# The last tile stored in two halves by two queues, and the tile before it finished earlier

## Chip, core and metric

One NeuronCore of a Trainium2 chip runs the whole program. The metric is device time in microseconds of one execution, as the median of several runs. Engines named below: TensorE (matrix products), VectorE, ScalarE, GpSimd, and SyncE (SP), which here only starts DMAs. Each engine works through its own queue of instructions in order; they meet at semaphores, which one engine or DMA counts up and another waits for.

## What is computed

```python
w = weights[conditions]                        # (128, 32, 32), picked from 200
h = einsum('bct,bcd->bdt', x, w)               # x: (128, 32, 256), float32
u = square(relu(einsum('bsh,hi->bsi', h, up_w)))        # 256 -> 1024
shared = einsum('bsi,ih->bsh', u, down_w)               # 1024 -> 256
scale = top_k(einsum('bsh,he->bse', h, gate_w), 2).sum()
y = shared + einsum('bsh,hd->bsd', h, expert_weight) * scale
mu, var = mean(y), mean(square(y - mu))                 # over the 256
out = x + (y - mu) * rsqrt(var + 1e-5) * gamma + beta
```

The 128 x 32 rows of x are 4096 tokens of 256 numbers.

## The kernel before, in words

The 4096 tokens are 32 groups of 128 rows (`GROUPS`); four of them make a block (`TILES`, `BLOCKS` = 8). A group is also called tile n, n = 4 * block + t, with n from 0 to 31. TensorE runs blocks in a pipeline: while block j is projected up (`up`, L385), block j-1 is projected down (`down`, L406). There is a last pass, j = `BLOCKS`, with `down` alone: it does two halves for each of the tiles 28 to 31, after the late half of tile 27. Products are made in float32 out of a rounded part and a rest, which is why each operand has a `_hi` and a `_lo`.

What follows a `down` on the other engines, for each tile:

- VectorE, `total` (L571): waits for the matmuls (`down_done`), adds the two halves of the result and the expert part (L581, L584), and takes statistics with L587. For the very last tile everything is already summed in PSUM, so `total` is only the statistics, straight from `down_ps` (L576).
- VectorE, `moments` (L589): aggregates the statistics (L597) and centres and scales by gamma (L603), into `y[t % 2]`.
- GpSimd, `inverse_std` (L689): waits for L597 and raises the variance to the power -0.5 (L692), into `rstd[t % 2]`.
- VectorE, `finish` (L606): waits for L603 and L692 and makes the result with L614, into `result[:, j % 2, t, :]`, and counts `result_done` up.
- SP stores the result. Blocks 0 to 6 go out as a whole, 512 KB (`store`, L277). Block 7 goes out tile by tile, 128 KB each: L290 waits for `result_done` to reach n + 1, L291 starts the DMA. The order is fixed, tile 28, 29, 30, 31.

VectorE's order is written by hand in the loop at L646 to L668. For blocks 0 to 6, `finish` of a tile follows its own `moments`. For block 7 it is one tile behind: `moments` of tile t is followed by `finish` of t - 1, so VectorE doesn't stand and wait for GpSimd. The last `finish` (tile 31) is behind the loop, L669. Just ahead of it stands, at L666, `finish` of tile 30, after the statistics and the centring of tile 31.

ScalarE's part ends with `scale_moe` of the last tile (L533). At the end SP waits until all stores have landed (L292, L293; `result_moved`, one semaphore each for even and odd blocks), and the block is closed: every engine counts up a semaphore, and all leave together (L46).

Of the kernel before, what the change touches and what calls it, by code (L numbers as in the profile page):

```python
# [5 lines left out]
P = 128  # L6
# [29 lines left out]
def adaln_ffn(nc, x, cond, cond_w, gate_w, up_w, down_w, expert_w, gamma, beta, out):  # L36
# [9 lines left out]
    with ctx:  # L46
# [71 lines left out]
        wd_second_landed = [sem("wd_second_landed_sp"), sem("wd_second_landed_pool")]  # L118
        wd_landed = {j: sem(f"wd_landed_block{j}") for j in range(2, BLOCKS)}
        result_moved = [sem("result_moved_even"), sem("result_moved_odd")]  # L120


        warm_ready, consts_ready = map(sem, ("warm_ready", "consts_ready"))
# [108 lines left out]
        @block.sync  # L232
        def _(sp):
            def load_down(load):
                n = CH // DOWN_LOADS
                part = slice(n * load, n * (load + 1))
                sp.dma_start(down_raw[:, part, :], down_rows[:, part, :]).then_inc(down_landed[load], 16)

            cond_flat = cond.rearrange("(o b) -> o b", o=1)
            sp.dma_start(cond_row[:, 0:TILES * Q], cond_flat[:, 0:TILES * Q]).then_inc(cond_first_landed, 16)  # L240
            sp.dma_start(cond_row[:, TILES * Q:ROWS_B], cond_flat[:, TILES * Q:ROWS_B]).then_inc(cond_later_landed, 16)
            sp.wait_ge(cond_first_landed, 16)
            values = conditions(mybir.EngineType.SP, range(0, HALF_BLOCK))
            sp.wait_ge(wd_zeroed[0], 1)
            for b in BY_SP:
                sp.dma_start(square_of(b), weights_of(values[b])).then_inc(wd_first_landed[b // Q], 16)
            values = conditions(mybir.EngineType.SP, range(HALF_BLOCK, 2 * HALF_BLOCK))
            for b in BY_SP_LATER:
                sp.dma_start(square_of(b), weights_of(values[b])).then_inc(wd_later_landed[0], 16)
            load_up(sp, 2)  # L250
            sp.dma_start(eg_raw[:, :, 0:T], expert_w.rearrange("(k p) h -> p k h", p=P)).then_inc(eg_landed, 16)
            sp.dma_start(eg_raw[:, :, T:EG], gate_w.rearrange("(k p) e -> p k e", p=P)).then_inc(eg_landed, 16)
            sp.dma_start(x_sb[:, groups(1), :], x_rows[:, groups(1), :]).then_inc(x_landed[1], 16)
            sp.wait_ge(cond_later_landed, 16)
            second = range(TILES * Q, TILES * Q + HALF_BLOCK)
            values = conditions(mybir.EngineType.SP, second)
            sp.wait_ge(wd_zeroed[1], 1)
            for b, value in values.items():
                sp.dma_start(square_of(b), weights_of(value)).then_inc(wd_second_landed[0], 16)
            load_down(0)  # L260
            load_down(1)
            sp.dma_start(beta_b[:, :], beta.rearrange("(o t) -> o t", o=1).to_broadcast([P, T])) \
                .then_inc(ln_landed, 16)
            sp.dma_start(gamma_b[:, :], gamma.rearrange("(o t) -> o t", o=1).to_broadcast([P, T])) \
                .then_inc(ln_landed, 16)

            def fetch(j):
                if TILES * (j + 1) > GROUPS - CH:

                    sp.wait_ge(down_lo_ready, DOWN_PARTS)  # L270
                sp.dma_start(x_sb[:, groups(j), :], x_rows[:, groups(j), :]).then_inc(x_landed[j], 16)
                batches = range(TILES * Q * j, TILES * Q * (j + 1))
                values = conditions(mybir.EngineType.SP, batches)
                for b, value in values.items():
                    sp.dma_start(square_of(b), weights_of(value)).then_inc(wd_landed[j], 16)

            def store(j):  # L277
                sp.wait_ge(result_done, TILES * j + TILES)
                sp.dma_start(out_rows[:, groups(j), :], result[:, j % 2, :, :]).then_inc(result_moved[j % 2], 16)

            for j in range(2, BLOCKS - 2):
                fetch(j)
            store(0)
            for j in range(BLOCKS - 2, BLOCKS):
                fetch(j)
            for j in range(1, BLOCKS - 1):
                store(j)
            for t in range(TILES):
                n = TILES * (BLOCKS - 1) + t
                sp.wait_ge(result_done, n + 1)  # L290
                sp.dma_start(out_rows[:, n:n + 1, :], result[:, 1, t:t + 1, :]).then_inc(result_moved[1], 16)  # L291
            sp.wait_ge(result_moved[0], 16 * (BLOCKS // 2))  # L292
            sp.wait_ge(result_moved[1], 16 * (BLOCKS // 2 - 1 + TILES))  # L293

# [173 lines left out]
        @block.scalar  # L468
        def _(act):
            def hidden(j, k):  # L470
                act.wait_ge(hid_done, rounds(j, k))
                act.activation(hid_hi[:, j % 2, k, :], round_bank(j, k)[:, :], ACT.Copy).then_inc(hid_hi_done, 1)

            def hidden_first(half, k):
                act.wait_ge(hid_done, K * half + k + 1)
                act.activation(hid_hi[:, 0, k, half_tok(half)], first_bank(half, k)[:, 0:HALF_TOK], ACT.Copy) \  # L476
                    .then_inc(hid_hi_done, 1)

            def scale_moe(j, t):
                n = TILES * j + t  # L480
                act.wait_ge(scale_done, n + 1)
                to = moe_hl[:, 0, :] if last_tile(j, t) else moe[:, j % 2, t, :]
                act.activation(to, moe_ps[:, 0:T], ACT.Copy, scale=scale[:, t % 2:t % 2 + 1]) \  # L483
                    .then_inc(moe_scaled, 1)

            def rectify(j, c):
                n = CH * j + c
                act.wait_ge(up_done, n + 1)

                wait(act, square_done, n - 1)  # L490
                act.activation(relu[:, c % 2, :], up_ps[c % UPB][:, :], ACT.Relu).then_inc(relu_done, 1)  # L491
                act.wait_ge(relu_done, n + 1)
                act.activation(sq_hi[:, j % 2, c, :], relu[:, c % 2, :], ACT.Square).then_inc(sq_hi_done, 1)  # L493

            def split_up(part):
                act.wait_ge(up_landed[part], 16)
                act.activation(up_hi[:, :, split_cols(part)], up_raw[:, :, split_cols(part)], ACT.Copy) \
                    .then_inc(up_hi_ready, 1)

            def split_down(part):  # L500
                act.wait_ge(down_landed[part * DOWN_LOADS // DOWN_PARTS], 16)
                act.activation(down_hl[:, down_chunks(part), 0, :], down_raw[:, down_chunks(part), :], ACT.Copy) \
                    .then_inc(down_hi_ready, 1)


            act.activation(table_loaded[:, :], nc.const_aps.tensor(0.0, [P, 1], f32), ACT.Copy)
            load_x_first(act, 0)
            load_up(act, 0)
            act.wait_ge(cond_first_landed, 16)
            values = conditions(mybir.EngineType.Activation, range(0, HALF_BLOCK))  # L510
            act.wait_ge(wd_zeroed[0], 1)
            for b in BY_ACT:
                act.dma_start(square_of(b), weights_of(values[b])).then_inc(wd_first_landed[b // Q], 16)  # L513
            split_up(0)
            load_up(act, 1)
            load_x_first(act, 1)
            hidden_first(0, 0)
            hidden_first(0, 1)
            split_up(1)
            hidden_first(1, 0)  # L520
            hidden_first(1, 1)
            act.wait_ge(eg_landed, 32)
            act.activation(eg_hi[:, :, :], eg_raw[:, :, :], ACT.Copy).then_inc(eg_hi_ready, 1)
            for j in range(BLOCKS):
                for c in range(CH):
                    for moe_block, t in scaled_at(j, c):
                        scale_moe(moe_block, t)
                    for k in rounds_at(j, c - 1):
                        hidden(j + 1, k)
                    rectify(j, c)  # L530
                    for part in SPLIT_DOWN_AT.get(c, ()) if j == 0 else ():
                        split_down(part)
            scale_moe(BLOCKS - 1, TILES - 1)  # L533

        @block.vector
        def _(dve):
# [109 lines left out]
            for j in range(BLOCKS + 1):  # L646
                for c in range(CH):
# [12 lines left out]
                    for block, t in tiles_at(j, c):  # L660
                        moments(block, t)

                        if block < BLOCKS - 1:
                            finish(block, t)
                        elif t > 0:
                            finish(block, t - 1)  # L666
                    for part in SPLIT_DOWN_AT.get(c, ()) if j == 0 else ():
                        split_down(part)  # L668
            finish(BLOCKS - 1, TILES - 1)  # L669
# [77 lines left out]
```

## Time and profile before

| | us |
|---|---|
| median of 3 runs | 230.31 (230.11 to 230.64) |
| the profiled execution, its own time | 230.09 |
| its span, first to last instruction | 228.5 |

| engine | busy us | share of the span |
|---|---|---|
| TensorE, matmul | 221.8 | 97% |
| TensorE, weight load | 191.9 | 84% |
| VectorE | 162.2 | 71% |
| GpSimd | 130.5 | 57% |
| ScalarE | 105.7 | 46% |

TensorE's granted clock was at its full level for the whole span but its last fractions of a microsecond, behind the last matmul. The busy times are averages over the whole span; the last microseconds look different, since there TensorE has nothing left to do. A start and a duration in the rows are microseconds from the start of the span; `<-` stands between what an instruction writes and what it reads.

### The profile page before, as it was taken

To read this page: it belongs to the slowest core of one execution; us is meant where nothing else is said; L and a number is where in the kernel's file an instruction comes from. 1 tells how busy PE (TensorE), PEld (TensorE's weight loads), DVE (VectorE), ACT (ScalarE), POOL (GpSimd) and SP (SyncE) were. 2 spreads that over 40 slices of the span, in tenths; PEclk is the share of its full clock that TensorE was granted. 3 is DMA by queue.
4 is the path that set the end of the run, shared out by engine and by line. 5 is a ranking of instruction groups with operands and counts; after the bars stand their busy time and mean duration, and the time that the engine had idled before them with its cause. 6 is when DMAs were issued, how large, how long until landed. Compare 5 with 4: busy or idle time off the path is not lost.

```text
span 228.5 us, 3998 instructions
## 1 busy us (share of the span) xinstructions
PE 221.8 (97%) x1260; PEld 191.9 (84%) x1260; DVE 162.2 (71%) x352; ACT 105.7 (46%) x187; POOL 130.5 (57%) x131
## 2 busy tenths in 40 slices
PE   7999999999999999999999999999999999999992
PEld 2888888988898888888888888888888888888892
DVE  6486975877667877667677766587766766777884
ACT  3378944444455355444545435534454444444000
POOL 3748776575536663656555664366555575557411
PEclk9999999999999999999999999999999999999999
DMA  3867123030503011000200002000020002000021
GB/s 98 239 205 227 41 68 102 8 99 7 185 11 98 9 43 53 0 0 3 92 0 0 3 0 95 0 3 0 0 95 1 0 0 71 25 0 0 19 99 69
DMA packets 17177, 11.81 MB, mean 52 GB/s; under 512 B 6660, under 2 KB 16900, under 8 KB 17156
## 3 DMA queue, kind: packets, MB, share of 16 engines
q1 hardware_dynamic: 15460, 10.43, 15.2%
q10 hardware_dynamic: 1280, 1.07, 1.5%
q8 instruction: 10, 0.16, 0.3%
q0 software_dynamic: 416, 0.05, 0.2%
q14 instruction: 11, 0.09, 0.1%
HBM read 7.35 MB, written 4.19 MB: 51 GB/s over the span
## 4 chain that ended last, share of the span: by engine, by line
PE 93%; DVE 2%; DMA 1%; issue 1%; ACTq 1%; ACT 0%; DVEq 0%
PE up_ps L337 38%; PE down_ps L431 25%; PE down_ps L433 13%; PE hid_ps L303 5%; PE moe_ps L447 3%; PE moe_ps L449 3%; PE moe_ps L448 3%; DMA wd<-in_L_cond_weights_dram 1%; ACTq L513 1%; PE down_ps L303 1%; DVE up_lo L619 1%; DMA cond_row<-in_itok_B_dram 1%; PE down_ps L429 0%; PE down_ps L427 0%; PE down_ps L428 0%
## 5 line engine op out<-in xcount | busy, mean ns | idle before, releaser
L677 POOL TENSOR_TENSOR sq_lo<-square,sq_hi 128x512 fp32r<-128x512 f32 x64 | 83.6, 1310 | 78.6 <-DVE square L552 77.4
L431 PE MATMUL down_ps<-down_hl,sq_hi 128*128 128x512 f32 x248 | 88.8, 393 | 0.0
L433 PE MATMUL down_ps<-down_hl,sq_lo 128*128 128x256 f32 x248 | 69.6, 280 | 0.0
L552 DVE SCALAR_TENSOR_TENSOR square<-up_ps,relu 128x512 f32<-128x512 f32 x64 | 43.8, 686 | 35.7 <-ACT relu L491 26.2
L431 PEld LDWEIGHTS down_ps<-down_hl,sq_hi 128*128 128x128 f32 x248 | 46.5, 188 | 10.8 <-issue 0.3
L491 ACT ACTIVATE relu<-up_ps 128x512 f32<-128x512 f32 x64 | 38.1, 595 | 33.5 <-PE up_ps L337 33.5
L337 PE MATMUL up_ps<-hid_hi,up_hi 128*128 128x512 f32 (+1 forms) x136 | 52.8, 391 | 0.7 <-ACT hid_hi L476 0.3
L337 PE MATMUL up_ps<-hid_hi,up_lo 128*128 128x512 f32 (+1 forms) x136 | 51.1, 379 | 0.0
L433 PEld LDWEIGHTS down_ps<-down_hl,sq_lo 128*128 128x128 f32 x248 | 46.7, 188 | 2.4
L493 ACT ACTIVATE sq_hi<-relu 128x512 fp32r<-128x512 f32 x64 | 40.5, 633 | 2.0
L337 PE MATMUL up_ps<-hid_lo,up_hi 128*128 128x512 f32 (+1 forms) x136 | 40.6, 381 | 0.0
L483 ACT ACTIVATE moe<-moe_ps,scale 128x256 f32<-128x256 f32 x31 | 14.7, 475 | 50.8 <-DVE scale L562 50.8
L337 PEld LDWEIGHTS up_ps<-hid_lo,up_hi 128*128 128x128 f32 x136 | 24.9, 188 | 5.4
L337 PEld LDWEIGHTS up_ps<-hid_hi,up_hi 128*128 128x128 f32 x136 | 25.6, 188 | 4.3 <-issue 1.0
L337 PEld LDWEIGHTS up_ps<-hid_hi,up_lo 128*128 128x128 f32 x136 | 25.6, 188 | 2.6
L603 DVE SCALAR_TENSOR_TENSOR y<-y,meanvar,gamma_b 128x256 f32<-128x256 f32 x31 | 26.6, 858 | 1.1
L692 POOL TENSOR_TENSOR rstd<-meanvar,minus_half 128x1 f32<-128x1 f32 x32 | 20.4, 639 | 11.6 <-DVE meanvar L597 11.6
L614 DVE SCALAR_TENSOR_TENSOR result<-y,rstd,x_sb 128x256 f32<-128x256 f32 x32 | 15.4, 483 | 12.2 <-POOL rstd L692 12.2
L686 POOL TENSOR_TENSOR x_sb<-x_sb,beta_b 128x512 f32<-128x512 f32 x16 | 20.7, 1294 | 0.0
L447 PE MATMUL moe_ps<-eg_lo,hid_hi 128*128 128x264 f32 x64 | 18.3, 286 | 0.0
L449 PE MATMUL moe_ps<-eg_hi,hid_hi 128*128 128x264 f32 x64 | 18.2, 284 | 0.0
L448 PE MATMUL moe_ps<-eg_hi,hid_lo 128*128 128x264 f32 x64 | 18.2, 284 | 0.0
(62 smaller groups left out, 195.6 us busy)
## 6 DMA issues: line engine op xcount, KB each, us to landing
x_sb<-in_x_dram SPq DMA_DIRECT2D x7, 512.0 KB, 4.3
out_dram<-result SPq DMA_DIRECT2D x7, 512.0 KB, 3.1
wd<-in_L_cond_weights_dram SPq DMA_DIRECT2D x111, 4.0 KB, 1.6
x_sb<-in_L_ffn_down_w_dram SPq DMA_DIRECT2D x2, 512.0 KB, 4.4
x_sb<-in_x_dram ACTq DMA_DIRECT2D x2, 256.0 KB, 3.0
result<-in_L_ffn_up_w_dram ACTq DMA_DIRECT2D x2, 256.0 KB, 2.9
result<-in_L_ffn_up_w_dram SPq DMA_DIRECT2D x1, 512.0 KB, 4.6
out_dram<-result SPq DMA_DIRECT2D x4, 128.0 KB, 1.7
```

Source lines behind the costliest of these rows:

```text
L337: return pe.matmul(up_ps[c % UPB][:, cols], w[:, k, P * c:P * c + P], h[:, j % 2, k, cols], start=(n == 0), stop=(n == 3 * K - 1))
L431: pe.matmul(dst[:, :], a_hi, down_hl[:, c, :, :].rearrange("p s t -> p (s t)"), start=(c == 0), stop=False)
L433: mm = pe.matmul(dst[:, T:2 * T], a_lo, down_hl[:, c, 0, :], start=False, stop=(c == CH - 1))
L447: pe.matmul(dst, a_hi, eg_lo[:, k, :], start=(k == 0), stop=False)
L448: pe.matmul(dst, a_lo, eg_hi[:, k, :], start=False, stop=False)
L449: mm = pe.matmul(dst, a_hi, eg_hi[:, k, :], start=False, stop=(k == K - 1))
L491: act.activation(relu[:, c % 2, :], up_ps[c % UPB][:, :], ACT.Relu).then_inc(relu_done, 1)
L493: act.activation(sq_hi[:, j % 2, c, :], relu[:, c % 2, :], ACT.Square).then_inc(sq_hi_done, 1)
L552: dve.scalar_tensor_tensor(square[:, c % 2, :], up_ps[c % UPB][:, :], 0.0, relu[:, c % 2, :], ALU.max, ALU.mult).then_inc(square_done, 1)
L603: dve.scalar_tensor_tensor(y[:, t % 2, :], total_y, meanvar[:, t % 2, 0:1], gamma_b[:, :], ALU.subtract, ALU.mult).then_inc(centred, 1)
L677: pool.tensor_tensor(sq_lo[:, j % 2, c, :], square[:, c % 2, :], sq_hi[:, j % 2, c, :].bitcast(f32), ALU.subtract).then_inc(sq_lo_done, 1)
L686: pool.tensor_tensor(x_sb[:, part, :], x_sb[:, part, :], beta_b[:, :].unsqueeze(1).to_broadcast([P, 2, T]), ALU.add).then_inc(xb_done, 1)
```

## The change

Two things, both for block 7 only. First, the store of tile 31 is made of two DMAs: rows 0 to 63 from SP, as before in the loop, and rows 64 to 127 from ScalarE, which waits for `result_done` to reach 32 behind its last work. The second half has a semaphore of its own, `last_half_moved`, and SP waits for that too at the end. Second, `finish` of tile 30 is called right behind `moments` of tile 30, ahead of `total` and `moments` of tile 31. Instructions on TensorE and GpSimd are unchanged.

```diff
+        last_half_moved = sem("last_half_moved")
@@ SP
             for t in range(TILES):
                 n = TILES * (BLOCKS - 1) + t
+                rows = slice(0, P // 2) if t == TILES - 1 else slice(0, P)
                 sp.wait_ge(result_done, n + 1)
-                sp.dma_start(out_rows[:, n:n + 1, :], result[:, 1, t:t + 1, :]).then_inc(result_moved[1], 16)
+                sp.dma_start(out_rows[rows, n:n + 1, :], result[rows, 1, t:t + 1, :]).then_inc(result_moved[1], 16)
+            sp.wait_ge(last_half_moved, 16)
             sp.wait_ge(result_moved[0], 16 * (BLOCKS // 2))
             sp.wait_ge(result_moved[1], 16 * (BLOCKS // 2 - 1 + TILES))
@@ ScalarE
             scale_moe(BLOCKS - 1, TILES - 1)
+            act.wait_ge(result_done, TILES * BLOCKS)
+            act.dma_start(out_rows[P // 2:P, GROUPS - 1:GROUPS, :], result[P // 2:P, 1, TILES - 1:TILES, :]) \
+                .then_inc(last_half_moved, 16)
@@ VectorE
                         if block < BLOCKS - 1:
                             finish(block, t)
-                        elif t > 0:
+                        elif 0 < t < TILES - 1:
                             finish(block, t - 1)
+                            if t == TILES - 2:
+                                finish(block, t)
```

## Rows read from the trace of the kernel before

**Rows 1.** The page's chain that ended last, by engine

```profile
PE 93%; DVE 2%; DMA 1%; issue 1%; ACTq 1%; ACT 0%; DVEq 0%
```

**Rows 2.** Timeline of VectorE near the end: start us, duration us, line, operation, out<-in

```profile
215.30 0.48 DVE L614 SCALAR_TENSOR_TENSOR result<-y,rstd,x_sb 128x256 f32<-128x256 f32 x1 [0.51 <-POOL rstd L692]
...
223.23 0.47 DVE L614 SCALAR_TENSOR_TENSOR result<-y,rstd,x_sb 128x256 f32<-128x256 f32 x1
224.22 0.43 DVE L576 BATCH_NORM_STATS2 stats<-down_ps 128x6 f32<-128x256 f32 x1 [0.52 <-PE down_ps L429]
224.92 0.48 DVE L603 SCALAR_TENSOR_TENSOR y<-down_ps,meanvar,gamma_b 128x256 f32<-128x256 f32 x1
225.32 0.87 DVE L614 SCALAR_TENSOR_TENSOR result<-y,rstd,x_sb 128x256 f32<-128x256 f32 x2
```

**Rows 3.** The same for GpSimd

```profile
214.35 0.84 POOL L692 TENSOR_TENSOR rstd<-meanvar,minus_half 128x1 f32<-128x1 f32 x1 [0.28 <-DVE meanvar L597]
...
222.84 0.55 POOL L692 TENSOR_TENSOR rstd<-meanvar,minus_half 128x1 f32<-128x1 f32 x1 [2.22 <-DVE meanvar L597]
...
224.96 0.55 POOL L692 TENSOR_TENSOR rstd<-meanvar,minus_half 128x1 f32<-128x1 f32 x1 [1.57 <-DVE meanvar L597]
```

**Rows 4.** The same for SP's queue, issues of L291

```profile
220.96 0.35 SPq L291 DMA_DIRECT2D out_dram<-result  x1
223.72 0.35 SPq L291 DMA_DIRECT2D out_dram<-result  x1
225.82 0.33 SPq L291 DMA_DIRECT2D out_dram<-result  x1
226.22 0.41 SPq L291 DMA_DIRECT2D out_dram<-result  x1
```

**Rows 5.** The page's DMA issues: count, KB each, median us from issue to landing

```profile
out_dram<-result SPq DMA_DIRECT2D x4, 128.0 KB, 1.7
```

**Rows 6.** DMA view of 226.2 to 229: busy tenths in slices of 0.07 us

```profile
DMA  0000002899894489997400000000000000000000
...
out_dram<-result SPq DMA_DIRECT2D x1, 128.0 KB, 1.8
```

**Rows 7.** Instructions of line L293: duration ns, first and last start us

```profile
L293 SPq EVENT_SEMAPHORE  x1: 17/17/17, 228.0 to 228.0; - x1
```

**Rows 8.** Instructions of line L46, SP's branch

```profile
L46 SPq COMPARE_BRANCH  x1: 33/33/33, 228.1 to 228.1; - x1
```

**Rows 9.** Windows: us, busy time by engine, granted clock, DMA share, GB/s

```profile
221.80:221.90 0.10, 0.10 (x3) 0.10 (x2) 0.10 (x1) 0.00 (x0) 0.00 (x0) 1.00 0.56 205
221.90:222.20 0.30, 0.30 (x5) 0.30 (x4) 0.27 (x2) 0.00 (x0) 0.00 (x0) 1.00 0.96 338
222.20:222.40 0.20, 0.20 (x5) 0.20 (x4) 0.20 (x1) 0.00 (x0) 0.00 (x0) 1.00 0.16 46
```

**Rows 10.** Timeline of ScalarE, its last instruction with work

```profile
212.82 0.47 ACT L483 ACTIVATE moe_hl<-moe_ps,scale 128x256 fp32r<-128x256 f32 x1 [2.42 <-DVE scale L562]
```

**Rows 11.** Line L246, 4 KB loads from SP: duration ns, and us to landing

```profile
L246 SPq DMA_DIRECT2D wd<-in_L_cond_weights_dram x4: 315/324/350, 3.1 to 4.6; - x4
...
DMA to landing us min/median/max: 1.5/1.7/1.8
```

**Rows 12.** Line L513, 4 KB loads from ScalarE, in the same form

```profile
L513 ACTq DMA_DIRECT2D wd<-in_L_cond_weights_dram x4: 347/362/388, 3.1 to 4.6; - x4
...
DMA to landing us min/median/max: 1.7/1.9/2.1
```

**Rows 13.** Line L228, 256 KB loads from ScalarE, in the same form

```profile
L228 ACTq DMA_DIRECT2D x_sb<-in_x_dram x2: 433/462/492, 1.0 to 5.5; - x2
...
DMA to landing us min/median/max: 2.9/3.0/3.2
```

**Rows 14.** Windows near the start, columns as above

```profile
1.80:2.00 0.20, 0.20 (x1) 0.00 (x0) 0.20 (x1) 0.20 (x1) 0.00 (x0) 1.00 0.01 0
2.00:2.10 0.10, 0.10 (x2) 0.06 (x1) 0.10 (x1) 0.10 (x1) 0.00 (x0) 1.00 0.14 51
```

## The prediction

> **What bounds the kernel now.** I read the chain that ended last first: 93% of the span is TensorE [rows 1]. The change touches no TensorE instruction, so it can only act behind the last matmul or in what that matmul waits for. So the rest of the reading stays in the last 6 us.
>
> Next, VectorE's timeline of the end [rows 2]. The last matmul is done by 224.2 us. Behind it stand five VectorE steps: the statistics of tile 31 (L576) at 224.22, their aggregate, the centring (L603) at 224.92, and two L614 back to back, at 225.32 for tile 30 and then for tile 31. The pair is booked as 0.87 us from 225.32, so the second ends at 226.19, and with 0.48 for one it starts at 225.71. GpSimd's power step (L692), which the second needs, runs from 224.96 to 225.51 [rows 3].
>
> Then SP's queue [rows 4]: the store of tile 30 is issued at 225.82 (0.33), that of tile 31 at 226.22 (0.41), each 0.03 after its L614 ended. SP was free from 226.15, so the last issue waited for VectorE and not for SP. The stores land 1.7 us after the issue in the median [rows 5]; for the last one it is 1.8 [rows 6]. That gives 226.22 + 1.8 = 228.02, and the wait on L293 wakes at 228.0 [rows 7]. SP's branch follows at 228.1 [rows 8] and the span ends at 228.5. So the tail behind TensorE is 4.3 us: 2.0 on VectorE with the hand-over, 1.8 of store, 0.5 of closing.
>
> **Part 1, tile 30 is finished before tile 31's statistics.** Nothing is added or removed; one L614 moves from 225.32 to behind tile 30's own L603.
> - Where it lands: the L614 of tile 29 starts at 223.23. Two in a row start 0.39 apart (225.32, 225.71), so tile 30's can start at 223.62. Its power step ended at 222.84 + 0.55 = 223.39 [rows 3], and an L614 that waits for this step follows its end by 0.11 us (214.35 + 0.84 = 215.19, start 215.30) [rows 2, 3]; so 223.50 is early enough. It ends at 223.62 + 0.48 = 224.10, inside the gap of 0.52 that VectorE has until tile 31's statistics at 224.22 [rows 2]. The cover is that wait for TensorE, with 0.1 to spare; beyond it every tenth would be paid in full, because tile 31's statistics are queued behind. Bounds: 0 and 0.39, the latter if none were hidden. I take 0.
> - What it frees: the last L614 has no other ahead of it. What is late next is GpSimd: 225.51 + 0.11 gives a start at 225.62. So the start moves from 225.71 to 225.62 only, not by a whole L614; the end moves from 226.19 to 226.10, the issue from 226.22 to 226.13. A gain of 0.09 (bounds 0 and 0.12).
> - The moved step's store: tile 30's is issued at about 224.13 instead of 225.82. SP holds tile 29's issue from 223.72 for 0.35, to 224.07 [rows 4], so it waits for nothing. Today the last two tiles' packets are on the engines one behind the other with a dip but no pause between them [rows 6]; a tile that is alone (tile 28) needs only 221.80 to 222.40 [rows 9]. Afterwards tile 30 is off the engines by 225.6 and tile 31 goes alone. A whole store would then land after 1.7 like the others, not 1.8: a gain of 0.1 (bounds 0 and 0.1).
>
> **Part 2, tile 31's store in two halves, one from ScalarE.** It adds an issue on ScalarE's queue, a wait of ScalarE on the last L614, and one of SP on the new half. ScalarE's last work starts at 212.82 [rows 10]; nothing stands behind its wait but the closing, which waits for SP anyway.
> - Issue: an SP issue costs 0.32 for 32 rows of 128 B [rows 11] and 0.33 to 0.35 for 128 rows where it isn't close behind another [rows 4], so it scarcely goes with rows; ScalarE's costs 0.36 for the small form [rows 12]. Halving the rows buys 0 to 0.02.
> - Transfer: in both cases 128 rows of 1 KB go through the same 16 engines. A whole tile keeps them at 0.96 over 221.90 to 222.20, at 338 GB/s [rows 9]; two queues can't add to that. The first packets come 0.84 after the issue (220.96 to 221.80) [rows 4, 9]. A 4 KB load on SP lands in 1.5 to 1.8 [rows 11], a 128 KB store in 1.7 [rows 5]; so the best bound for a half is 1.5.
> - ScalarE's queue: of equal 4 KB loads, four each issued side by side, ScalarE's land after 1.7, 1.9 and 2.1 (least, median, most) against 1.5, 1.7 and 1.8 on SP [rows 11, 12]. Its queue is 0.2 slower there. It has also been idle since 5.5 us; its first use was issued at 1.0 and the first packets of any weight came in 2.00 to 2.10, some 0.2 later than the 0.84 above [rows 13, 14]. The worst landing of this queue at all is 3.2, for 256 KB [rows 13]. No row shows a store from ScalarE. Between 1.5 and 2.1 I take 1.8 for the later half: SP's 1.7, with half of the queue's 0.2 on it and no saving for the smaller transfer. That eats the 0.1 which part 1 won on the transfer.
> - Closing: SP has one wait more. The wake on L293 and the next instruction stand 0.1 apart [rows 7, 8]; a wait that comes behind the landing costs up to that, one ahead of it nothing. I take 0.05.
>
> The rows show issues of 0.32 and 0.33 for 32 and 128 rows. The Trainium skill, page "DMA: Bandwidth & Descriptors", section "Issuing engines are not separate DMA queues", says that DMAs of several issuers interleave on the same 16 engines and that starting them at once only saves the time of initiating them. An estimate by that rule, if the issue shrank with the rows, would be half of 0.33 to 0.41, so 0.2 off the sum below. The trace doesn't bear even that out.
>
> **Sum.** The last landing was 226.22 + 1.8 = 228.02 and becomes 226.13 + 1.8 = 227.93: minus 0.09. The wait adds 0.05. Net minus 0.04 us. The profiled execution took 230.09 with a span of 228.5, so 1.6 lies around the span and stays; it would be 230.05. That execution is 0.22 below the median of the three timed runs, 230.31, and just under their lowest, 230.11. Against the median the forecast is 230.27; I give 230.25.
>
> **Rivals.**
> 1. The forecast: gains and costs of a tenth each, next to nothing left. For it: every term is bounded by a row, and only the last store has ends far apart. Chance 0.70.
> 2. The split pays: both halves land like the quickest small loads, 1.5 after the issue. Then 226.13 + 1.5 = 227.63, minus 0.39, with 0.05 for the wait minus 0.34: 229.97. For it: the 4 KB rows on SP. Against: those of ScalarE, and engines that one tile already fills. Chance 0.13. Even this lies inside 0.2% (0.46 us), about what a measurement of this kernel can tell from no change; only with the spread of the runs on its side does it go past it.
> 3. Slower: ScalarE's half is late, because its queue has been idle for 220 us or because two queues hold up each other's completions on full engines. It decides from a landing of 228.02 + 0.46 - 0.05 = 228.43, that is 2.3 after the issue; the slowest small transfer of that queue took 2.1 and its 256 KB loads up to 3.2 [rows 12, 13]. At 2.6, in between, the last landing is at 228.73, so the time is 230.31 + 0.71 + 0.05 = 231.07. For it: no row shows a store on that queue. Against: it needs more than the worst small row. Chance 0.09.
> 4. Tile 30's L614 is not covered: its power step takes 0.84, as at 214.35 [rows 3], instead of 0.55. Then it starts at 222.84 + 0.84 + 0.11 = 223.79 and ends at 224.27, and tile 31's statistics come 0.1 late. The gain of part 1 is gone: 230.31 + 0.05, so 230.4, which is the same within 0.2%. Chance 0.08.
>
> **How the numbers follow.** Faster by over 0.2%: 0.05 from rival 2 and 0.02 from the spread of the runs (230.11 to 230.64) on the first, together 0.07. Slower by over 0.2%: 0.07 from rival 3 and 0.02 from the same spread, 0.09. The rest, 0.84, is within 0.2%. The range goes from minus 0.34 (rival 2) to plus 0.31 (ScalarE's half at 2.1 and the wait at 0.1: 226.13 + 2.1 - 228.02 + 0.1) around the median, 229.97 to 230.62, and by 0.15 more on either side for the spread of the runs: 229.8 to 230.75.
>
> **What would show it.** Part 1: an L614 at about 223.6, statistics of tile 31 still right behind the last matmul, one L614 alone at 225.62 with the power step named as its releaser. Part 2: issues of both queues at about 226.13, packets between 226.97 and 227.5 and none from 225.6 to 226.9, landings of 1.7 (SP) and 1.8 (ScalarE), the closing branch at 228.0. I am wrong if the statistics of tile 31 start more than 0.1 behind the matmul, if ScalarE's landing is below 1.6 or above 2.2, or if another engine reaches the closing later than SP does.

## The result and the profile after

The changed kernel takes 230.70 us (22 runs, 230.32 to 231.03) and the kernel before 230.32 us (22 runs, 230.03 to 230.79). The ratio is 1.0015, with an interval from 1.0009 to 1.0021: 0.35 us slower, inside the 0.2% that the prediction called no change, but a loss beyond doubt, where the forecast was 0.06 us faster.

The two profiled executions are 230.09 before and 230.95 after, with spans of 228.5 and 229.2. This difference is larger than that of the medians, since the one execution lies 0.2 below its median and the other 0.25 above. To compare tails I use a stretch that contains the change and little else: from the start of tile 31's statistics (L576, now L583) to the end of the span, read to two digits from the traces. Before, that is 228.47 - 224.22 = 4.25 us. After, it is 229.24 - 224.65 = 4.59 us. The 0.34 of difference is the 0.35 of the timed runs.

VectorE's timeline of the changed kernel (start us, duration us, line; L610 is the centring, L621 the result step):

```profile
223.66 0.87 DVE L621 SCALAR_TENSOR_TENSOR result<-y,rstd,x_sb 128x256 f32<-128x256 f32 x2
224.65 0.43 DVE L583 BATCH_NORM_STATS2 stats<-down_ps 128x6 f32<-128x256 f32 x1
...
225.35 0.48 DVE L610 SCALAR_TENSOR_TENSOR y<-down_ps,meanvar,gamma_b 128x256 f32<-128x256 f32 x1
226.04 0.48 DVE L621 SCALAR_TENSOR_TENSOR result<-y,rstd,x_sb 128x256 f32<-128x256 f32 x1 [0.21 <-POOL rstd L702]
```

It answers to [rows 2]. Tiles 29 and 30 are now finished as a pair at 223.66, and the statistics follow the last matmul as before: there is no idle time booked in front of L583 any more, yet it starts 0.99 behind the first of the pair, as before (223.23 to 224.22). The cover held. Of the last L621, the bracket says that it waited for the power step. From the statistics it starts after 1.39 us, where it was 225.71 - 224.22 = 1.49.

The issues of both queues, one timeline each:

```profile
226.55 0.55 SPq L294 DMA_DIRECT2D out_dram<-result  x1
...
226.56 0.58 ACTq L539 DMA_DIRECT2D out_dram<-result  x1
```

These answer to the last line of [rows 4], where the issue took 0.41 and, in the three before it, 0.33 to 0.35. Half the rows take longer to issue. Two pieces of the DMA view, the packets of 226.5 to 228.0 and then of 228.0 to 228.6 (q1 is SP's queue, q10 ScalarE's; the issue lines give KB and us to landing):

```profile
q1 hardware_dynamic: 44, 0.05, 12.1%
out_dram<-result SPq DMA_DIRECT2D x1, 64.0 KB, 2.0
out_dram<-result ACTq DMA_DIRECT2D x1, 64.0 KB, 2.3
...
q10 hardware_dynamic: 80, 0.07, 42.3%
q1 hardware_dynamic: 36, 0.02, 14.8%
```

Up to 228.0 there is not one packet of ScalarE's queue. Windows of the same stretch (the last two numbers are the DMA share and GB/s):

```profile
226.50:227.70 1.20, 0.00 (x0) 0.00 (x0) 0.03 (x1) 0.00 (x0) 0.00 (x0) 1.00 0.00 0
227.70:228.00 0.30, 0.00 (x0) 0.00 (x0) 0.00 (x0) 0.00 (x0) 0.00 (x0) 1.00 0.61 150
```

Nothing moves until 227.7, which is at least 1.15 us after the issues; the kernel before had first packets after 0.84. The second half then lands at 226.56 + 2.3 = 228.8, and SP's branch, at 228.1 in [rows 8], is now at 228.8. That landing, 2.28 us after the issue, is beyond the 2.2 that the prediction had named as a sign of being wrong.

### The profile page after: what moved, and what is told of

It is laid out like the page before. It is cut to its first block, busy times and chain, and to the rows that moved or that the text cites. A ratio compares the mean times of both kernels' runs of the same rounds, so it can differ in the third digit from the quotient of the medians.

```text
span 229.2 us, 3999 instructions
## 1 busy us (share of the span) xinstructions
PE 221.8 (97%) x1260; PEld 191.7 (84%) x1260; DVE 162.4 (71%) x352; ACT 105.8 (46%) x187; POOL 130.4 (57%) x131
## 4 chain that ended last, share of the span: by engine, by line
PE 90%; DMA 3%; DVE 2%; SPq 2%; issue 1%; POOLq 0%; POOL 0%; DVEq 0%
PE up_ps L341 36%; PE down_ps L435 25%; PE down_ps L437 13%; PE hid_ps L307 5%; PE moe_ps L451 3%; PE moe_ps L453 3%; PE moe_ps L452 3%; DMA result<-in_L_ffn_up_w_dram 2%; SPq L247 1%; SPq L210 1%; DVE up_lo L626 1%; DMA cond_row<-in_itok_B_dram 1%; SPq L250 0%; PE down_ps L307 0%; DVE up_hi L648 0%
## 5 line engine op out<-in xcount | busy, mean ns | idle before, releaser
L610 DVE SCALAR_TENSOR_TENSOR y<-y,meanvar,gamma_b 128x256 f32<-128x256 f32 x31 | 26.6, 857 | 1.1
L621 DVE SCALAR_TENSOR_TENSOR result<-y,rstd,x_sb 128x256 f32<-128x256 f32 x32 | 15.4, 484 | 12.5 <-POOL rstd L702 12.5
```

The costliest lines, as they stand in the source:

```text
L610: dve.scalar_tensor_tensor(y[:, t % 2, :], total_y, meanvar[:, t % 2, 0:1], gamma_b[:, :], ALU.subtract, ALU.mult).then_inc(centred, 1)
```

## Experiments

All expectations were written before the kernels ran. Three explanations of the late landing stood against each other. A: two queues that issue at the same moment hold each other up. B: ScalarE's queue is slow, by itself or because it was idle for 220 us. C: a DMA of 64 rows is slow by itself. "Tail" is the stretch defined above.

**Each part alone.** The first kernel keeps only the reorder, the second only the split.

```diff
 reorder_only: kernel before, plus
-                        elif t > 0:
+                        elif 0 < t < TILES - 1:
                             finish(block, t - 1)
+                            if t == TILES - 2:
+                                finish(block, t)
```

> The earlier finish of tile 30 alone, tile 31 stored whole by SP. All theories agree that the two parts of the change are separate. The tail from the start of tile 31's statistics to the end of the span was 4.25 us before and 4.59 after the change. Here the last result step ends 0.09 earlier than before, and tile 31's store is alone on the engines, so it should land 1.7 us after its issue and not 1.8. Expected tail 4.05 to 4.10, time 0.15 to 0.2 below before, ratio 0.9992. If the tail is 4.25 or more, the reorder gains nothing and the rest of my account falls too.

```diff
 split_only: changed kernel, minus
-                        elif 0 < t < TILES - 1:
+                        elif t > 0:
                             finish(block, t - 1)
-                            if t == TILES - 2:
-                                finish(block, t)
```

> Tile 31 in two halves from SP and ScalarE, VectorE's order as before. All of the loss belongs to the split, whatever its cause: landings of 2.0 (SP) and 2.3 (ScalarE) again, issue 0.1 later than with the reorder, tail 4.70. Where tile 30's store, issued 0.4 earlier, also costs the halves something, up to 4.85. Ratio 1.002 to 1.0025. If it lands like a whole store (1.8), the loss comes from the two parts together.

The reorder alone: 230.06 against 230.36, ratio 0.999 (0.998 to 1.000), tail 4.07. The split alone: 230.77 against 230.36, ratio 1.0019 (1.0007 to 1.0030), tail 4.68. So one part brings some 0.2 us and the other costs 0.4 or more. The interval of the reorder ends at 1.000, so its gain is clear in the trace's steps and only just in the timed runs. VectorE and SP of the kernel with the reorder alone:

```profile
223.62 0.47 DVE L614 SCALAR_TENSOR_TENSOR result<-y,rstd,x_sb 128x256 f32<-128x256 f32 x1
224.22 0.43 DVE L576 BATCH_NORM_STATS2 stats<-down_ps 128x6 f32<-128x256 f32 x1
...
225.61 0.48 DVE L614 SCALAR_TENSOR_TENSOR result<-y,rstd,x_sb 128x256 f32<-128x256 f32 x1 [0.21 <-POOL rstd L694]
...
226.12 0.33 SPq L291 DMA_DIRECT2D out_dram<-result  x1
```

The forecast had 223.62, 225.62 and 226.13. Tile 31's store, whole and alone, lands after 1.7 (DMA view of 226 to 229 us):

```profile
out_dram<-result SPq DMA_DIRECT2D x1, 128.0 KB, 1.7
```

**One queue for both halves, and ScalarE for the whole.**

```diff
 both_halves_sp: changed kernel, ScalarE's store moved to SP, behind the first half
+                if t == TILES - 1:
+                    sp.dma_start(out_rows[P // 2:P, n:n + 1, :], result[P // 2:P, 1, t:t + 1, :]) \
+                        .then_inc(last_half_moved, 16)
```

> With the reorder; both halves of tile 31 from SP, one issue behind the other. Theory A (two queues that issue at the same moment hold each other up): nothing issues at the same moment, so each half lands 1.6 to 1.8 after its own issue; the second is issued 0.35 to 0.4 later, so the tail is 4.05 plus 0.3 to 0.4, some 4.4. Theory B (ScalarE's queue is slow by itself or because it was idle): the same 4.4, as ScalarE is not used. Theory C (a DMA of 64 rows is slower than one of 128 by itself): each lands 2.0 or more after its issue, tail 4.7.

```diff
 whole_scalar: changed kernel, SP's loop ends at tile 30
-            act.dma_start(out_rows[P // 2:P, ...], result[P // 2:P, ...])
+            act.dma_start(out_rows[0:P, ...], result[0:P, ...])
```

> With the reorder; tile 31 is stored whole by ScalarE, SP does not store it. Theory A (queues that issue at the same moment hold each other up): ScalarE issues alone, so issue about 0.4 us, landing 1.7 to 1.8, tail about 4.1, like the reorder alone. Theory B (ScalarE's queue is slow because it was idle for 220 us, or by itself): issue 0.55 or more, landing 2.1 to 2.3, tail 4.5. Theory C (64 rows): as A, since all 128 rows go in one.

Both halves from SP: 231.31 against 230.36, ratio 1.0034 (1.0020 to 1.0047), tail 4.95; that is more than any theory had said, because the longer first issue also holds back the second, which starts 0.60 behind it (L296 below, at 226.97) where the expectation had 0.35 to 0.4. ScalarE for the whole: 230.24, ratio 0.9997 (0.9985 to 1.0009), tail 4.06. Line L296 is the second half on SP, L539 is ScalarE's whole store (duration of the issue in ns, then us to landing):

```profile
L296 SPq DMA_DIRECT2D out_dram<-result x1: 587/587/587, 227.0 to 227.0; - x1
...
DMA to landing us min/median/max: 2.0/2.0/2.0
```

```profile
L539 ACTq DMA_DIRECT2D out_dram<-result x1: 373/373/373, 226.3 to 226.3; - x1
...
DMA to landing us min/median/max: 1.7/1.7/1.7
```

B falls: the queue that had been idle since 5.5 us issues in 0.373 and lands after 1.74, against 1.69 on SP. A can't explain the other: nothing was issued at the same moment as the 64 rows on SP, and still they take 0.587 and 2.0. C remains.

**A half alone.**

```diff
 sp_half_alone: changed kernel
-            act.wait_ge(result_done, TILES * BLOCKS)
-            act.dma_start(out_rows[P // 2:P, ...], result[P // 2:P, ...]).then_inc(last_half_moved, 16)
-            sp.wait_ge(last_half_moved, 16)
```

> The changed kernel without ScalarE's half: rows 64 to 127 of tile 31 are not stored, and nothing waits for them. Theory C: SP's half still takes 0.55 to issue and lands 2.0 after it although nothing else is on the engines; tail 4.05 plus 0.3, some 4.35 to 4.4. Theory A (the other queue holds it up): issue 0.33 to 0.35, landing 1.6 to 1.7, tail 4.05.

This kernel leaves rows 64 to 127 of tile 31 unstored. It and the three kernels that repeat stores further down were executed once each, so only their rows are read and not their time. The tail of this one is 4.37. SP's timeline, then two windows:

```profile
226.64 0.55 SPq L294 DMA_DIRECT2D out_dram<-result  x1
...
226.60:227.80 1.20, 0.00 (x0) 0.00 (x0) 0.01 (x1) 0.00 (x0) 0.00 (x0) 0.88 0.00 0
227.80:228.30 0.50, 0.00 (x0) 0.00 (x0) 0.00 (x0) 0.00 (x0) 0.00 (x0) 0.50 0.53 131
```

With 64 KB less to store than the kernel with the reorder alone its tail is 0.3 us longer. The first packets come 1.2 after the issue, and 64 KB take most of a window of 0.5 us, where 128 KB needed 221.80 to 222.40 [rows 9].

**Which shapes.** Behind the last store of the kernel with the reorder alone, SP stores parts of the result again, each behind the landing of the one before.

```diff
 shapes_sp: kernel with the reorder alone, at the end of SP's work
+            sp.dma_start(out_rows[0:P, GROUPS - 1:GROUPS, 0:T], result[0:P, 1, 3:4, 0:T]).then_inc(probe, 16)
+            sp.wait_ge(probe, 16)
+            sp.dma_start(out_rows[0:64, GROUPS - 1:GROUPS, 0:T], result[0:64, 1, 3:4, 0:T]).then_inc(probe, 16)
+            sp.wait_ge(probe, 32)
+            ...
```

> The kernel with the reorder alone, and behind its last store SP stores parts of tile 31 (and of its neighbours) again, one at a time, each behind the landing of the one before: 128, 64, 64 (upper), 128, 32, 96, 112, 48 and 16 rows of 1 KB; 128 and 64 rows of 512 B; 64 and 128 rows of 992 B; 64 rows of four tiles; 128 rows of two. The values stored are the same ones again. Theory C (a DMA of 64 rows is slow by itself): issue 0.55 and landing 2.0 for both row halves, 0.33 to 0.35 and 1.7 for the whole before and after them; the others show whether it goes with the number of rows (then 512 B and four tiles of 64 rows are slow too) or with the 64 KB that lie in one piece (then 64 rows of 992 B and of 512 B are as quick as 128). Theory A (only issues at the same moment are slow): all land in 1.7 or less.

SP's timeline, in the order of the expectation:

```profile
227.97 0.33 SPq L295 DMA_DIRECT2D out_dram<-result  x1
229.68 0.56 SPq L297 DMA_DIRECT2D out_dram<-result  x1
231.70 0.47 SPq L299 DMA_DIRECT2D out_dram<-result  x1
233.64 0.34 SPq L301 DMA_DIRECT2D out_dram<-result  x1
235.36 0.34 SPq L303 DMA_DIRECT2D out_dram<-result  x1
236.85 0.33 SPq L305 DMA_DIRECT2D out_dram<-result  x1
...
240.42 0.32 SPq L309 DMA_DIRECT2D out_dram<-result  x1
242.00 0.31 SPq L311 DMA_DIRECT2D out_dram<-result  x1
243.41 0.35 SPq L313 DMA_DIRECT2D out_dram<-result  x1
244.99 0.47 SPq L315 DMA_DIRECT2D out_dram<-result  x1
246.78 0.47 SPq L317 DMA_DIRECT2D out_dram<-result  x1
248.72 0.36 SPq L319 DMA_DIRECT2D out_dram<-result  x1
250.45 0.65 SPq L321 DMA_DIRECT2D out_dram<-result  x1
253.61 0.39 SPq L323 DMA_DIRECT2D out_dram<-result  x1
```

Whole before and after: 0.33 and 0.34, in slots of 1.71 and 1.72 us from issue to next issue. The row halves: 0.56 and 0.47, slots of 2.02 and 1.94. But 32, 96, 48 and 16 rows (L303, L305, L309, L311) are at 0.31 to 0.34 and in slots of 1.49, 1.70, 1.58 and 1.41. (112 rows, L307, took 0.32 to issue and landed after 1.9, which no theory had and nothing here explains.) 128 rows of 512 B (L313) take 0.35 and 1.58; 64 rows of 512 B (L315), a quarter of the tile, take 0.47 and 1.79. 64 rows of 992 B, which do not lie in one piece in memory, are just as slow (0.47, 1.94). And 64 rows of four tiles (L321), 256 KB, take 0.65 and 3.16, while 128 rows of two tiles (L323), the same 256 KB, take 0.39 and land after 2.2. So it goes neither with the number of bytes, nor with their lying in one piece, nor with having few rows.

```diff
 shapes_more: as above, with
+            80 rows; rows 32 to 95; 128; 56; 60; 68; 72; 120; 63; 8; 64 rows
+            sp.dma_start(x_sb[0:64, 0:1, :], x_rows[0:64, 0:1, :]).then_inc(probe, 16)   # and 0:P, 0:32
```

> Behind the last store of the kernel with the reorder alone, SP stores parts of tile 31 again, one at a time: 80 rows; rows 32 to 95; 128; 56; 60; 68; 72; 120; 63; 8; 64 rows. Then it loads 64, 128 and 32 rows of x into a tile that nobody reads any more. Theory C1 (64 rows as such): 80, 56, 60, 72 and 120 take 0.31 to 0.35 to issue and land like their neighbours of before (1.55 to 1.7); rows 32 to 95 and 0 to 63 take 0.47 and land 1.92 again; the load of 64 rows also takes 0.1 more to issue than those of 128 and 32. Theory C2 (four rows for each of the engines used, which 56 and 60 would give as well if the rows are dealt evenly over 14 and 15 engines): 56 and 60 are slow too, 1.9. Theory C3 (rows below 64 quick, 64 to 95 slow, 96 and more quick): 68, 72 and 80 are slow.

SP's timeline (80; 32 to 95; 128; 56; 60; then 64 rows; then the loads of 64, 128 and 32):

```profile
228.40 0.33 SPq L295 DMA_DIRECT2D out_dram<-result  x1
230.06 0.64 SPq L297 DMA_DIRECT2D out_dram<-result  x1
232.04 0.34 SPq L299 DMA_DIRECT2D out_dram<-result  x1
233.75 0.38 SPq L301 DMA_DIRECT2D out_dram<-result  x1
235.31 0.33 SPq L303 DMA_DIRECT2D out_dram<-result  x1
236.86 0.25 SPq L305 DMA_DIRECT2D out_dram<-result  x1
...
245.55 0.50 SPq L315 DMA_DIRECT2D out_dram<-result  x1
247.52 0.52 SPq L317 DMA_DIRECT2D x_sb<-in_x_dram  x1
249.64 0.38 SPq L319 DMA_DIRECT2D x_sb<-in_x_dram  x1
251.63 0.33 SPq L321 DMA_DIRECT2D x_sb<-in_x_dram  x1
```

80, 56 and 60 rows are quick (slots of 1.66, 1.56 and 1.55); 64 rows are slow at another start row too (0.64, slot 1.98) and the load of 64 rows is slow to issue (0.52; its slot of 2.12 is longer than the 1.99 of the load with twice the bytes). This is C1: 64 rows as such. With 56 and 60 quick C2 falls. 68, 72, 120, 63 and 8 rows took 0.25 to 0.33 to issue, so C3 falls too; but 120 rows came in a slot of 1.87, not 1.7, and 68 rows in one of 2.24. A late landing alone is therefore not special to 64 rows; the long issue is.

The DMA view tells more of these stores. A store of n rows shows n packets of 1 KB and some of 4 bytes; "under 512 B" counts the latter. The windows are those of the 56, the 68 and the last 64 rows:

```profile
DMA packets 70, 0.06 MB, mean 36 GB/s; under 512 B 14, under 2 KB 70, under 8 KB 70
...
DMA packets 72, 0.07 MB, mean 31 GB/s; under 512 B 4, under 2 KB 72, under 8 KB 72
...
DMA packets 80, 0.07 MB, mean 33 GB/s; under 512 B 16, under 2 KB 80, under 8 KB 80
```

Over all of them the small packets are 16 for 32 to 95, 0 to 63, 80 and 128 rows, 14 for 56, 15 for 60 and 120, 12 for 72, 9 for 63, 8 for 8 and 4 for 68. If each engine that takes part sends one at its end, they count the engines. Then 68 rows were late because 4 engines had 17 rows each, and 64 rows used all 16 engines and were slow all the same. 120 rows (15 engines, 8 rows each, like 128 rows on 16) stay unexplained.

**Pairs.** The same method with two queues.

```diff
 pairs: kernel with the reorder alone, at the end of SP's and of ScalarE's work; each waits for both landings
+            sp.dma_start(out_rows[0:64, ...], result[0:64, ...]).then_inc(probe_sp, 16)
+            act.dma_start(out_rows[64:P, ...], result[64:P, ...]).then_inc(probe_act, 16)
```

> The kernel with the reorder alone; behind its last store SP and ScalarE issue stores together, each pair behind the landing of the pair before: a whole tile each; row halves; column halves (128 rows of 512 B each); 32 rows each; then alone, one at a time: whole by SP, whole by ScalarE, row half by SP, row half by ScalarE. The values stored are the same ones again. Theory C alone (the shape is all): halves by rows land alike alone and in pairs, 2.0 to 2.05, and whole tiles in a pair land 1.7 plus their 0.35 of shared transfer. Theory A and C together: the pair of row halves lands 0.2 to 0.3 after its single stores (2.0 and 2.3, as in the changed kernel), and the pair of 128-row column halves also shows a ScalarE landing 0.2 or more above 1.75. Column halves in a pair: 1.7 by C alone, 1.9 to 2.0 by both.

ScalarE's row half in the pair (L563) and alone (L579):

```profile
L563 ACTq DMA_DIRECT2D out_dram<-result x1: 569/569/569, 230.0 to 230.0; - x1
DMA to landing us min/median/max: 2.3/2.3/2.3
...
L579 ACTq DMA_DIRECT2D out_dram<-result x1: 482/482/482, 241.7 to 241.7; - x1
DMA to landing us min/median/max: 1.9/1.9/1.9
```

The pair of row halves landed after 2.0 and 2.3, as in the changed kernel; alone the same half took 1.9. Column halves landed after 1.6 (SP) and 1.8, whole tiles after 1.8 and 2.1 against 1.7 alone, 32 rows after 1.5 and 1.7. So A is true too, beside C: of two issues at one moment the second queue's lands 0.2 to 0.4 later than alone, and SP's by 0.1 or less. (For columns and for 32 rows "alone" is SP's store in the first of the two kernels above, 1.56 and 1.48; none was made from ScalarE.) Whole tiles share the engines' time, but the row halves show that it is not only that: ScalarE's first packet comes 1.48 after its issue in the pair and 1.14 alone. The expectation for the column halves was missed: 1.8 where A with C said 1.9 to 2.0. In every pair ScalarE's issue was also the later one, by 0.004 to 0.013 us; whether the later issue or ScalarE's queue is held back was not tried.

**Other cuts on the same place.**

```diff
 rows_96_32: changed kernel
-                rows = slice(0, P // 2) if t == TILES - 1 else slice(0, P)
+                rows = slice(0, 96) if t == TILES - 1 else slice(0, P)
-            act.dma_start(out_rows[P // 2:P, ...], result[P // 2:P, ...])
+            act.dma_start(out_rows[96:P, ...], result[96:P, ...])
```

> The changed kernel with its cut by rows at 96 and not at 64: 96 rows from SP, 32 from ScalarE, issued together. The rest is the same instruction for instruction. If the 64-row shape is the cause: issues of 0.33 to 0.38, SP's landing 1.7, ScalarE's 1.6 to 1.8, tail 4.05 to 4.15, ratio 0.999 to 0.9995. If a cut by rows or two row parts on two queues were the cause: as the changed kernel, tail 4.6, ratio 1.0015.

```diff
 column_halves: changed kernel
-                rows = slice(0, P // 2) if t == TILES - 1 else slice(0, P)
+                cols = slice(0, T // 2) if t == TILES - 1 else slice(0, T)
-            act.dma_start(out_rows[P // 2:P, ..., :], result[P // 2:P, ..., :])
+            act.dma_start(out_rows[0:P, ..., T // 2:T], result[0:P, ..., T // 2:T])
```

> The changed kernel with tile 31 cut by columns and not by rows: 128 rows of 512 B from SP and 128 rows of 512 B from ScalarE, issued together. Theory C (rows below 128 are slow): issues of 0.35 to 0.4 and landings of 1.7 to 1.8, tail 4.1, ratio 0.9992 to 0.9995. Theory A and C together: ScalarE's landing 1.95 to 2.0, tail 4.3, ratio 1.000. Theory A alone: as the changed kernel, 2.3, tail 4.6.

```diff
 early_columns: as column_halves, and in finish, for tile 31
+                    for h, counted in enumerate((first_cols_done, result_done)):
+                        part = slice(T // 2 * h, T // 2 * (h + 1))
+                        dve.scalar_tensor_tensor(result[..., part], y[..., part], rstd[...], x_sb[..., part],
+                                                 ALU.mult, ALU.add).then_inc(counted, 1)
 and SP's half of tile 31 waits for first_cols_done
```

> Cut by columns as before, and the last result step is made in two column halves too, so that SP's half is issued before ScalarE's. The first half's result should end 0.15 to 0.2 earlier than the whole one, the second 0.05 to 0.15 later. ScalarE's store then stands almost alone: 1.6 to 1.65 after its issue and not 1.78. Expected tail 4.05 to 4.15, no gain on the kernel with the reorder alone (4.07), ratio 0.999. A tail below 4.0 would make it the best version.

| kernel | us | before, same chip | ratio (interval) | tail, us |
|---|---|---|---|---|
| cut at row 96 | 230.52 | 230.46 | 0.9999 (0.9989 to 1.0009) | 4.28 |
| column halves | 230.18 | 230.40 | 0.9988 (0.9979 to 0.9997) | 4.09 |
| early columns | 230.13 | 230.46 | 0.9984 (0.9973 to 0.9994) | 4.04 |

The cut at 96 takes the 64-row shape away and changes little else: SP's issue is 0.33 again, and 0.31 of tail comes back. What stays is the second queue's delay, which I had put too low: ScalarE's 32 rows take 0.374 to issue and land after 2.0, not 1.6 to 1.8. SP's 96 rows landed after 1.8. Column halves land after 1.6 and 1.8, and their tail of 4.09 is the 4.1 that the expectation gave to C alone, not the 4.3 of A with C. This does not clear A: a column half alone lands after 1.56, so ScalarE's is still 0.2 late. With early columns SP is issued 0.27 ahead, and ScalarE's store then lands like a single one:

```profile
226.42 0.33 SPq L298 DMA_DIRECT2D out_dram<-result  x1
...
226.68 0.37 ACTq L543 DMA_DIRECT2D out_dram<-result  x1
```

It landed after 1.59. Its tail is 0.02 below that of the reorder alone (4.043 and 4.067, from the traces); the intervals of the two ratios, 0.9984 and 0.999, overlap. In tail both are some 0.2 us ahead of the kernel before and 0.5 ahead of the changed one. The reorder alone is the simpler of the two and needs no second queue.

## Why the prediction was right or wrong

**Part 1 was right in every time that it named.** The moved L614 was put at 223.62 to 224.10 and came at 223.62 in the kernel with the reorder alone; the statistics were not delayed (224.22). The last L614 was put at 225.62 and came at 225.61; the issue at 226.13 came at 226.12. The landing after 1.7 and not 1.8 is there as well. Forecast for this part 0.19, measured 4.25 - 4.07 = 0.18. Half of it, the landing after 1.7 instead of 1.8, I put down to engines free of tile 30's packets. The issue itself also took 0.33 instead of 0.41 once it did not stand close behind another, and that 0.08 is nearly the whole 0.09 by which the landing came closer; which of the two it was is not shown. The last link, that an L614 follows the power step by 0.11, held (225.51 to 225.61), and rival 4 did not occur.

**The closing was on the wrong side, and small.** I took 0.05 for a wait behind the landing. In the changed kernel one of the waits sits on SP's branch itself, and the wait that stood between landing and branch is passed earlier, at 228.6. SP's waits show it (us in total, times, longest):

```profile
SPq L297 <- DMA out_dram<-result: 1.5, 1, 1.5
...
SPq L46 <- DMA out_dram<-result: 0.2, 1, 0.2
```

Between the last landing and the end of the span are 0.41 us and not 0.47. A gain of 0.06 in place of a loss of 0.05.

**The term that was mis-sized is the landing of the later half**: 1.8 taken, from 1.5 to 2.1, and 2.3 measured. This alone turns minus 0.04 into what came out: 2.28 for 1.78 is plus 0.49, the issue minus 0.09, the closing minus 0.06, together plus 0.34 (4.59 - 4.25 is the same). Two steps of its working failed.
- That an SP issue "scarcely goes with rows", from 32 rows of 128 B (0.32) and 128 rows (0.33 to 0.35), so that halving them buys 0 to 0.02. Both ends were quick, and 64 rows in between take 0.47 to 0.64. Interpolation was the mistake: the trace of before had no DMA of 64 rows. Two quick ends did not bound what lies between. Alone, this shape costs 0.2 to 0.3 us against the whole tile on SP (1.92 to 2.00 for 1.70), and 0.2 on ScalarE (1.94 for 1.73).
- That ScalarE's "queue is 0.2 slower there", from two series of loads side by side [rows 11, 12]. The whole tile from ScalarE lands after 1.7. So the 0.2 was no property of the queue. Most likely it was that of two queues issuing at once, but the loads of [rows 11, 12] were not run apart. I halved it because I took it for something else. In the pair of row halves it is 2.3 against 1.9.

Together: 1.69 for the whole tile on SP, 0.05 for ScalarE in its place, 0.20 for the 64 rows, 0.32 for the pair, 2.26; measured 2.28.

**Rival 3** had the sign and the place right. Of its two reasons the idle queue was wrong; two queues at once was right in part, though the engines were not full when ScalarE's half was late; and it did not name the 64-row shape. Its threshold of 2.3 after the issue for a loss of 0.46 fits what came: 2.28 and, with the closing 0.11 better than assumed, 0.35. **Rival 2**, that the smaller transfer pays, holds alone and for other shapes than 64 rows: 128 rows of 512 B land after 1.56, 48 rows after 1.56 and 32 rows after 1.48. In a pair ScalarE's later landing takes this back.

The Trainium skill, page "DMA: Bandwidth & Descriptors", section "Issuing engines are not separate DMA queues", had warned that two issuers share the engines and save only the issue time. The trace goes further: the second queue had not one packet before 228.0, 1.4 us after its issue, although the engines stood free until 227.7. In "Why a DMA increments its semaphore by 16 and not by 1" the page says that the largest number of engines up to 16 that divides the rows is used. By that 64, 80, 96 and 128 rows use 16 engines alike. The small packets above agree with it: 16 for 64, 80 and 128 rows, 14 for 56, 15 for 60, 4 for 68. So nothing in that rule sets 64 apart, and the measurement does.

**What stays open** is why 64 rows are slow. The runs show it for stores on both queues, for 1024, 992 and 512 B, for starts at rows 0, 32 and 64, and for one load; they show that both the issue and the time to the first packet grow (for stores 0.33 to 0.47 or more, 0.84 to 1.1 or more). From row 0 or 64 the packets of 1 KB are slower too, 67 ns in the median and not 46, so that 64 KB are spread over 0.44 us where 128 KB take 0.52; for rows 32 to 95 they took 45 and only the start was late. Nothing in the traces says what differs inside. Nor is it shown why the first 64-row issue of a kernel takes 0.55 to 0.64 and the later single stores 0.47 to 0.50; nor why 112 and 120 rows land late. The start of the tail differs by 0.43 us between the two profiled executions. That is scatter between executions: four kernels that are the same up to there (the reorder alone and the three that repeat stores behind it) start it at 224.21, 224.22, 224.30 and 224.73.

## What to carry to other kernels

Before a DMA at the end of a kernel is cut, look whether its time is transfer or fixed: here 1.2 of 1.7 us passed before the first and after the last packet (0.83 and 0.35), and cutting did not shorten that (16 rows still landed after 1.4), while two issues at one moment lengthened it. Where a cut is made at all, cut by columns, keep away from 64 rows, and stagger the issues, though none of the cuts here beat the whole store clearly (4.04 for 4.07 of tail); the better step here was to bring the result forward instead, since moving one step out of the last chain gave 0.18 us for no new instruction. And an unseen shape is no point between two seen ones: give it its own row or a wide range.

## What was not expected of the hardware

- A store of 64 rows (partitions) takes 0.47 to 0.65 us to issue, one of 16, 32, 48, 56, 60, 80, 96, 112 or 128 rows 0.31 to 0.39 where it does not stand close behind another issue (0.41 to 0.43 there); 64 rows of 1 KB land after 1.9 to 2.0, 128 rows after 1.7, 96 rows after 1.7, but 112 rows after 1.9; 256 KB as 64 rows of four tiles 3.1, as 128 rows of two tiles 2.2.
- Of two DMAs issued within 0.02 us by SP and ScalarE, ScalarE's (always the later issue) lands 0.2 to 0.4 later than alone, and SP's 0 to 0.1. 32 rows beside 96 came 0.5 later (1.96 for the 1.48 of SP alone).
- 68 rows sent 4 small packets and took a slot of 2.24 us, 72 rows sent 12 and took 1.64.
- A queue that was idle for 220 us is not slower: 0.373 to issue and 1.7 to land.
